# Causal attention: where future keys are masked, and which engine fills constant rows

## What is computed

```python
scores = einsum('bqhd,bkhd->bhqk', q, k) + einsum('bqr,bkr->bqk', q_rope, k_rope)[:, None]
scores = scores / sqrt(HD + D_R)                 # 8 + 32
scores = where(triu(ones(T, T), k=1), -inf, scores)
w = softmax(scores, axis=-1)                     # 16 heads, T = 1024
attn = einsum('bhqk,bkhd->bqhd', w, v).reshape(B, T, 128)
x = x + attn @ W_o
```

## Time and profile before

| | us |
|---|---|
| median of three runs | 2236.16 |
| the profiled execution | 2238.34 |
| span of its profile | 2236.5 |
| PE busy | 1811.4 |
| DVE busy | 1420.2 |
| ACT busy | 1165.3 |
| POOL busy | 469.3 |

### The profile page before, as it was taken

How to read it: one execution, slowest core, us unless ns; L and a number is a source line. 1 busy time by engine, 2 the same in 40 slices (tenths; PEclk the granted TensorE clock), 3 DMA queues, 4 the chain that set the end, 5 groups by cost and what they waited for, 6 DMA issues and landing times. The chain is left out here.

```text
span 2236.5 us, 42505 instructions
## 1 busy us (share of the span) xinstructions
PE 1811.4 (81%) x15621; PEld 967.5 (43%) x15621; DVE 1420.2 (63%) x2865; ACT 1165.3 (52%) x2304; POOL 469.3 (21%) x609
## 2 busy tenths in 40 slices
PE   3589999999999742998355999999999996339982
PEld 1245656666665432776231222222222222337751
DVE  4476666666665259541057999999999993584510
ACT  1316566666666410333152888888888885003330
POOL 1010000000000101688750000000000000017886
PEclk9769999999999955799676999999999998557996
DMA  3753652644440010343331000000000000014334
GB/s 105 212 104 55 111 106 47 113 82 77 88 72 2 1 40 25 86 69 61 30 132 61 16 18 29 16 21 26 16 24 23 16 2 17 25 29 95 60 59 64
DMA packets 97485, 124.79 MB, mean 56 GB/s; under 512 B 14696, under 2 KB 57584, under 8 KB 97264
## 3 DMA queue, kind: packets, MB, share of 16 engines
q1 hardware_dynamic: 72336, 104.59, 20.2%
q0 software_dynamic: 24960, 17.68, 6.1%
HBM read 87.17 MB, written 35.95 MB: 55 GB/s over the span
## 5 line engine op out<-in xcount | busy, mean ns | idle before, releaser
L982 DVE TENSOR_REDUCE mx<-wide 128x2 f32<-128x1024 f32 x512 | 603.6, 1221 | 52.4 <-PE wide L914 40.4
L1010 ACT ACTIVATE pT<-bank 128x512 f32<-128x512 f32 x1024 | 555.2, 595 | 85.7 <-PE bank L907 78.1
L743 ACT ACTIVATE pT<-bank 128x512 f32<-128x512 f32 (+3 forms) x768 | 358.9, 490 | 266.1 <-PE bank L610 248.0
L907 PE MATMUL bank<-q_st,k_st 51*128 51x512 bf16 x1024 | 355.3, 387 | 21.4 <-ACT pT L1010 5.4
L914 PE MATMUL wide<-k_st,q_st 48*128 48x512 bf16 x1024 | 351.9, 399 | 24.1 <-DVE mx L982 12.9
L712 DVE TENSOR_REDUCE mx<-wide 128x1 f32<-128x640 f32 (+3 forms) x256 | 259.1, 1023 | 133.2 <-PE wide L621 131.1
L923 PE MATMUL bank<-pT,vst 128*32 128x256 f32 x4096 | 328.3, 392 | 0.1
L610 PE MATMUL bank<-q_st,k_st 122*128 122x512 f32 (+3 forms) x768 | 314.4, 412 | 4.0 <-ACT pT L743 1.8
L621 PE MATMUL wide<-k_st,q_st 120*128 120x512 f32 (+3 forms) x768 | 312.4, 413 | 1.9 <-DVE mx L712 1.0
L907 PEld LDWEIGHTS bank<-q_st,k_st 51*128 51x128 bf16 x1024 | 91.6, 93 | 315.7 <-ACT pT L1010 272.9
L1473 POOL DMA_INDIRECT acc_rows<-yg,idxs x128 | 200.5, 1566 | 52.4 <-issue 36.6
(11 more groups left out here) (226 smaller groups left out, 2011.8 us busy)
## 6 DMA issues: line engine op xcount, KB each, us to landing
q_st<-rope_split SPq DMA_DIRECT2D x72, 256.0 KB
k_st<-rope_split SPq DMA_DIRECT2D x72, 256.0 KB
qk_split<-parts SPq DMA_DIRECT2D x8, 1024.0 KB, 8.1
q_st<-qk_split SPq DMA_DIRECT2D x96, 64.0 KB
k_st<-qk_split SPq DMA_DIRECT2D x96, 64.0 KB
qk_parts<-parts SPq DMA_DIRECT2D x8, 768.0 KB, 4.6
xn_rows<-xn SPq DMA_DIRECT2D x8, 512.0 KB, 3.2
w1b<-in_L_ffn_w SPq DMA_DIRECT2D x16, 256.0 KB, 2.9
```

What stands on the lines that cost most here:

```text
L743: e.activation(pT[:, u % NPB, q0:HALF], bank[u % 2][:, q0:HALF], ACT.Exp, scale=scale).then_inc(s_p, 1)
L907: e.matmul(bank[u % 2][:, :], k_st[at][64 * r:64 * r + KROW, jj, kc * P:(kc + 1) * P], q_st[at][64 * r:64 * r + KROW, jj, J * HALF:(J + 1) ...
L982: e.tensor_reduce(mx[G % 2][:, kh, pair:GH:2, c], wide[w % 2][:, :].rearrange("p (r k) -> p r k", r=2), AX.X, ALU.max).then_inc(s_sf, 1)
L1010: e.activation(pT[:, u % NPB, :], bank[u % 2][:, :], ACT.Exp, scale=scale).then_inc(s_p, 1)
```

## The change

The mask of the transposed tile (L608) is taken out. In its place GpSimd writes zeros into `pT` where the key is later than the query: one `affine_select` for the quad, over the first 128 columns of its four tiles, after their four exponentials and before the weighing, which waits for it. In GpSimd's order it stands first in step t = 2 quad + 2. The wait for the turned maximum and the DMA of its rows get a place of their own in that order, two steps after the turn. The fills of the constant rows of `k_st` 1 and 2 go from DVE to GpSimd, ahead of its fills of `vst`.

```diff
--- before.py
+++ after.py
@@ -549,7 +549,7 @@
             s_mch, s_m2, s_m = sem("split_chain"), sem("max_split"), sem("max_kept")
             s_st, s_p, s_pv = sem("t_tile"), sem("p_tile"), sem("pv")
             s_oev, s_ot, s_y, s_ych = sem("o_ev"), sem("o_turned"), sem("y"), sem("y_chain")
-            s_vz, s_vs = sem("v_init"), sem("v_stage")
+            s_vz, s_vs, s_cut = sem("v_init"), sem("v_stage"), sem("future_cut")
 
             buf, give_back = of_phase()
             stacks.grow(buf)
@@ -591,6 +591,15 @@
                 G, j, sides = score_at(w)
                 return next((side * HALF + HALF - P for side, (_, _, width, _) in enumerate(sides) if width < HALF), None)
 
+            def at_diagonal(quad):
+
+                s, J, kc, j, q0 = unit(quad * GH)
+                return kc >= J * CPH
+
+            def cuts_to(quad):
+
+                return sum(at_diagonal(n) for n in range(quad + 1))
+
             turns = {}
             for G in range(2 * STEPS):
                 w = begins(G + 1) + 2
@@ -598,18 +607,15 @@
                     w += 1
                 turns[min(w, LAST)] = (G, spare_of(w) if w < LAST else 0)
             ends = {begins(H + 1): H for H in range(2 * STEPS)}
+            kept_at = {(w if w < LAST else LAST + 2) - LEAD + 2: G for w, (G, col) in turns.items()}
             with nc.Block() as block:
                 @block.tensor
                 def _(e):
                     def t_score(u):
                         s, J, kc, j, q0 = unit(u)
-                        at, diag = s % NBUF, kc >= J * CPH
-                        if diag:
-                            e.matmul(bank[u % 2][:, q0:q0 + P], identb[:, :], mask_kq[:, :], start=True, stop=False,
-                                     skip_group_check=True)
+                        at = s % NBUF
                         e.matmul(bank[u % 2][:, q0:HALF], k_st[at][0:KROW, j, kc * P:(kc + 1) * P],
-                                 q_st[at][0:KROW, J, j, q0:HALF], start=not diag, stop=True,
-                                 skip_group_check=True).then_inc(s_st, 1)
+                                 q_st[at][0:KROW, J, j, q0:HALF], start=True, stop=True).then_inc(s_st, 1)
 
                     def score(w, side):
                         G, j, sides = score_at(w)
@@ -680,6 +686,7 @@
                             if t - 3 == begins(half_of(t - 3)) and half_of(t - 3) >= 2:
                                 e.wait_ge(s_y, PRIME + half_of(t - 3) - 1)
                             e.wait_ge(s_p, PRIME + (quad + 1) * GH)
+                            e.wait_ge(s_cut, PRIME + cuts_to(quad))
                             weigh(quad, 0)
                             weigh(quad, 1)
                         if t - 3 in ends:
@@ -691,9 +698,6 @@
 
                 @block.vector
                 def _(e):
-                    for k in k_st[1:]:
-                        e.memset(k[96:P, :, :].bitcast(F32), -1.0).then_inc(stacks.s_one, 1)
-
                     def keep_max(w):
                         G, col = turns[w]
                         if G >= 2:
@@ -750,6 +754,9 @@
 
                 @block.gpsimd
                 def _(e):
+                    for n, k in enumerate(k_st[1:]):
+                        e.memset(k[96:P, :, :].bitcast(F32), -1.0).then_inc(stacks.s_one, 1)
+                        e.wait_ge(stacks.s_one, n + 2)
                     for n, v in enumerate(vst):
                         e.memset(v[:, :, :, :], 0.0).then_inc(s_vz, 1)
                         e.wait_ge(s_vz, PRIME + n + 1)
@@ -760,6 +767,13 @@
                         e.tensor_copy(vst[s][:, :, :, 0:HD], v_all[:, s // NG, s % NG, :, :].rearrange("p c (j d) -> p c j d", j=GH)
                                       ).then_inc(s_vs, 1)
                     for t in range(-LEAD, LAST + 10):
+                        if t % 2 == 0 and 2 <= t <= LAST and at_diagonal(t // 2 - 1):
+                            quad = t // 2 - 1
+                            q0 = unit(quad * GH)[4]
+                            e.wait_ge(s_p, PRIME + (quad + 1) * GH)
+                            tiles = pT[:, quad * GH % NPB:quad * GH % NPB + GH, q0:q0 + P]
+                            e.affine_select(out=tiles, in_=tiles, compare_op=ALU.is_ge, fill=0.0, base=0,
+                                            pattern=[[0, GH], [1, P]], channel_multiplier=-1).then_inc(s_cut, 1)
                         if t + LEAD + 1 in ends:
                             G = ends[t + LEAD + 1]
                             e.wait_ge(s_sf, begins(G + 1))
@@ -768,6 +782,8 @@
                             e.tensor_copy(mx2[G % 2][:, 0, :].bitcast(F32R), mx[G % 2][:, :]).then_inc(s_mch, 1)
                             e.wait_ge(s_mch, PRIME + G + 1)
                             e.tensor_tensor(mx2[G % 2][:, 1, :], mx[G % 2][:, :], mx2[G % 2][:, 0, :], ALU.subtract).then_inc(s_m2, 1)
+                        if t in kept_at:
+                            G = kept_at[t]
                             e.wait_ge(s_m, PRIME + G + 1)
                             dst = q_st[G // 2 % NBUF][KS:KROW, G % 2, :, :].bitcast(F32)
                             e.dma_start(dst.rearrange("i j x -> i (j x)"), nmp[G % 2][:, :].bitcast(F32)).then_inc(s_row[G % 2], 16)
```

## The result

The changed kernel takes 2202.34 us (median of four runs, 2197.62 to 2204.54) against 2235.75 (four runs); the ratio is 0.9847, with a 95% interval of 0.983 to 0.9864. The forecast was 2204. The profiled execution took 2204.54 us with a span of 2202.8; it is the one to set against the 2238.34 before.

What follows compares the result with a forecast made beforehand. TensorE's order was taken as the bound, with ACT's release of banks second inside each quad. Masks -26.5, start -7.0 and end +1.0 gave -32.5 us, forecast 2204 us; 2197 to 2210 had chance 0.55, wider range 2190 to 2220.

Steps and rivals of the forecast that it cites:

- The masks: Diagonal quads on TensorE: removing the tile masks saves 1.77 us per stack over 15 stacks, -26.5 us.
- the two prices: Masks on TensorE: 0.12 us each where the tile's weight load could be hidden, 0.01 where it is exposed anyway.
- the prediction's other sum: All 512 masks on TensorE at one price, 56 ns each by the Trainium skill: 28.6 us.
- The select: GpSimd, each diagonal quad: one operation over 512 elements per partition, taken as 0.7 us, bounds 0.64 to 1.13.
- the lower bound of 0.64: Select on GpSimd: 0.28 us for 128 elements plus 384 more at 0.93 ns each, 0.64 us.
- The steady cost of 0: Steady part of a stack: selects end before their weighing needs them, so they cost 0.
- The tight place: 256 quad of a stack's first half: the select ends 0.5 us before its weighing, or 0.06 at the upper bound.
- The end: End of the attention: the last weighing waits for an uncovered select, +1.0 us, 0.7 to 1.4.
- The start: Before the first tile: constant-row fills moved off DVE let its reductions begin earlier, -7.0 us, bounds 0 and 10.
- The slower rival: Weighing: TensorE waits for long selects; decides from about 2.7 us, total 2287 us at 3.1; chance 0.07.

Runs made afterwards that it cites:

- the later division: The changed kernel with DVE's division of the output one step later, behind one more reduction: ratio 0.9805 to the kernel before.
- the masks put back at two of four tiles: The changed kernel with masks back at first and third tiles of each diagonal quad, then at second and fourth instead: 2209.22 and 2218.15 us.
- one fill: The changed kernel with one fill of 1024 elements on GpSimd ahead of each select: 2214.83 us.
- two fills: The changed kernel with two fills of 1024 elements on GpSimd ahead of each select: 2275.42 us, ratio 1.0174 to the kernel before.
- the old wait: The changed kernel with GpSimd's wait for the turned maximum and its DMA right behind the split, as before the change: 2371.59 us.
- no select: The changed kernel without GpSimd's select and the wait for it, so future keys of diagonal squares are weighed: 2197.32 us.
- maximum unmasked: The changed kernel with the masks of the maximum pass (L625) left out too: ratio 0.9702 to the kernel before.
- all together: The changed kernel with masks only at the last quad, none in the maximum pass, division one step later, values' copy two steps later: ratio 0.9692.
- the last quad by masks: The changed kernel with the last diagonal quad keeping its four masks and having no select: ratio 0.9839 to the kernel before.
- selects alone: The changed kernel with the fills of the constant rows back on DVE: 2207.14 us.

## Why the prediction was right

The forecast was 2204 us and 2202.34 was measured; the terms, as the traces have them, are these.

**The masks.** -26.5 foreseen, -28.3 found. The second is 1.96 us in each of 15 stacks, 29.4, less about 1 us in the last stack, where the clock fell for a moment (last section). Per quad on the diagonal, foreseen and found: second half 0.25 and 0.23, 0.16 and 0.20, 0.26 and 0.32, 0.31 and 0.34; first half 0.18 and 0.20, 0.08 and 0.10, 0.26 and 0.46, 0.27 and 0.11; in all 1.77 and 1.96 per stack. The distances of the earlier trace rows carried over to the hundredth. Two quads of the first half were off. The 256 quad gives 0.46 (3.64 to 3.18): its first mask stood behind the turning of the output (L689) and cost 0.11 there instead of 0.01, and c's load was hidden in full. The 128 quad gives 0.11, since DVE's division became the bound, a wait that the working had left out and the later division takes away. These two misses, +0.20 and -0.16, nearly cancel in the sum: there the forecast had luck. Nor does the total prove the two prices: the prediction's other sum, by one price for all 512 masks, is 28.6 us, nearer to 28.3 than 26.5 is. What tells the two apart are the distances, 0.12 and 0.01 in one quad, and the masks put back at two of four tiles, 0.42 and 1.07 us per stack.

**The select.** 0.7 taken, 0.635 found, which is the lower bound of 0.64 from the two small rows: from 128 to 512 elements it takes (635 - 284) / 384 = 0.91 ns for each one more, about the fill's 0.93. The steady cost of 0 holds: L642 never waits but at the end. The tight place had 0.67 us of room, where I had 0.46. One reading was wrong: the prediction said that no other quad has a split ahead of its select, but the 256 quad of the second half has one too, and its room is 0.76 us in most stacks, not the 1.5 to 2.2 of the six others. In the changed kernel that made no difference; it is the second of the two quads that one fill made late. By the Trainium skill (GPSIMD Engine Reference, Elementwise — side-by-side cycle accounting) branching by data costs about 12 cycles per element, which would be 5.1 us for 512 elements, an estimate from that figure at 1.2 GHz; that page does not name the select. The trace, with 0.635 us, disagrees by a factor of eight.

**The end.** +1.0 foreseen, +0.76 found; the handovers are 0.06 and 0.14 us.

**The start.** -7.0 foreseen, -7.19 found; GpSimd had 1.03 us to spare where I had 1.1. No load of stack 1 was a limit, as the whole gain arrives at the first tile and nothing of it is lost behind, and the clock rose no sooner than the rest moved: it is at 0.50 until the tiles have begun, and they begin 7.1 us earlier (145.0 for 152.1).

**The slower rival** had the right mechanism and a break-even somewhat too high. What it left out is that a late select can cost twice: behind the idle time TensorE ran at half clock in ten of the first fourteen stacks with two fills, and in every stack with the old wait.

## What to carry to other kernels

What an operation on TensorE costs is the change in the distance of starts around it, place by place; here it was 0.12 us where the weight load behind it could have been hidden and 0.01 where it could not; compare the same place with and without it in the trace that you have. Work moved to an idle engine cost nothing here as long as it ended before it was wanted, so list the engine's whole order, waits for others above all: here one wait left in its old place would have turned -33 us into +135. After each gain ask which engine's order has become the bound at that place; here the next 0.25 us per stack lay in DVE's.

## What the runs showed of the hardware

In the trace of the old wait the granted clock fell where a late weighing had left TensorE idle (busy 2.63 and 2.46 of 4 us), and it was at the lower level (1.2 GHz, 0.50) from 428 to 432 us although TensorE was busy throughout; in the next 4 us it is 0.63, in those behind 1.00. The clock also fell without any late select. In the last stack of the changed kernel, where no scores stand beside the tiles (busy time by stretch):

```profile
685.00:690.00 5.00, 4.10 (x42) 2.11 (x41) 0.28 (x1) 3.70 (x10) 2.56 (x5) 1.00 0.02 5
...
690.00:692.00 2.00, 1.72 (x10) 0.97 (x14) 0.00 (x0) 1.49 (x4) 0.12 (x2) 0.56 0.01 4
...
692.00:694.00 2.00, 2.00 (x18) 1.05 (x10) 0.00 (x0) 0.00 (x0) 0.59 (x1) 0.59 0.00 0
```

In the two stretches the clock is 0.56 and 0.59, means between its two levels of 1.2 and 2.4 GHz, which makes some 3.4 us at the lower one. One weighing takes 1.94 us instead of 1.07, and its quad 3.93 us; it is 2.97 in the kernel before, and 2.84 in the traces without masks whose clock does not fall there (no select, maximum unmasked, division later, all together). Against the trace with the division later the fall costs 1.3 us, in this quad and the one ahead of it. TensorE had been busy 4.10 of 5 us ahead of it. The trace with the last quad by masks has the same fall at the same place, the one with selects alone has one some 14 us later, and the kernel before (busy 4.48 of 5 us at this place, with its masks) has none. But the trace without selects is busy 4.11 of 5 us there and its clock stays at 1.00. So the missing masks do not bring the fall by themselves, and what does is not shown.
